# Graph and experts kernel: index loads reordered, routing laid into the first gather, gate applied by the experts' stage

## What is computed

```python
x = x + L0_gnn(layernorm(x))    # per edge: h[type, src] / deg[type, dst], summed at dst; + x @ W0.T + b
x = x + L0_ffn(layernorm(x))    # 8 experts, top 1, capacity 977, hidden 1024
x = x + L1_gnn(layernorm(x))    # graph convolution with normalised degrees, leaky relu
x = x + L1_ffn(layernorm(x))    # LSTM over the 6250 rows as one sequence, prefix and suffix sums
# L0_ffn, for each row:
probs = softmax(x @ gate_w + gate_b); idx = argmax(probs); prb = probs[idx]
pos = rank of the row among the rows of its expert; kept = pos < C
y = ybuf[idx, pos] * (prb * kept)          # ybuf = relu(buf @ w1 + b1) @ w2 + b2
y = nan_to_num(y, nan=0, posinf=10000, neginf=-10000)
```

## Time and profile before

| | us |
|---|---|
| median of 3 runs | 4495.27 (4494.93 to 4498.69) |
| the profiled execution | 4494.84 |
| its span | 4493.1 |
| PE / PEld busy | 3700.8 (82%) / 2830.6 (63%) |
| DVE / ACT / POOL busy | 1837.3 (41%) / 887.5 (20%) / 1631.3 (36%) |
| mean granted clock of TensorE | 0.879 |

### The profile page before, as it was taken

One profiled execution on the slowest core, in us unless ns is written; L12 is line 12 of the kernel. 1 busy time (PEld: TensorE's weight loads), 2 busy tenths in 40 slices (PEclk: granted clock), 3 DMA queues, 4 the chain that ended last, 5 costly groups with the idle time before them and its releaser, 6 DMA issues. The chain is left out here.

```text
span 4493.1 us, 64320 instructions
## 1 busy us (share of the span) xinstructions
PE 3700.8 (82%) x19849; PEld 2830.6 (63%) x19850; DVE 1837.3 (41%) x5512; ACT 887.5 (20%) x2492; POOL 1631.3 (36%) x1753
## 2 busy tenths in 40 slices
PE   3999999988878888865999865656667778999996
PEld 1444454457777777754666644555555557999996
DVE  3444420024334443444222283233344554444687
ACT  0333323310000000023111170000000002444453
POOL 1000000047777777733000036777777770000000
PEclk9999999978787777755999986788888899999998
DMA  4333333333333333332122054344455554433333
GB/s 156 121 120 123 125 116 149 147 117 111 110 110 111 111 111 110 111 122 90 62 82 80 28 158 133 107 126 136 148 152 161 174 183 156 148 111 115 108 108 107
DMA packets 213227, 545.38 MB, mean 121 GB/s; under 512 B 42897, under 2 KB 111358, under 8 KB 198119
## 3 DMA queue, kind: packets, MB, share of 16 engines
q1 hardware_dynamic: 121816, 297.98, 19.7%
q0 software_dynamic: 83344, 235.38, 17.8%
q10 hardware_dynamic: 7808, 8.92, 0.6%
HBM read 363.19 MB, written 178.51 MB: 121 GB/s over the span
## 5 line engine op out<-in xcount | busy, mean ns | idle before, releaser
L731 POOL DMA_INDIRECT a_msg<-scratch_hrel,k_rel_row x784 | 749.7, 956 | 1078.8 <-issue 1072.4
L1519 POOL DMA_INDIRECT b_msg<-scratch_gtab,k_src_row x784 | 763.2, 973 | 269.3 <-issue 263.5
L1568 PE MATMUL b_ps<-b_hit,b_msg 128*128 128x128 f32 x3136 | 492.6, 323 | 304.6 <-DMA b_msg<-scratch_gtab,k_src_row 296.4
L665 PE MATMUL r_psm<-k_w,r_xnT 128*128 128x512 f32 x1568 | 741.6, 609 | 0.9 <-ACT r_xnT L608 0.9
L834 PE MATMUL a_ps<-a_hit,a_msg 128*128 128x128 f32 x3136 | 562.9, 354 | 184.1 <-DMA a_msg<-scratch_hrel,k_rel_row 176.5
L1568 PEld LDWEIGHTS b_ps<-b_hit,b_msg 128*128 128x128 f32 x3136 | 460.9, 233 | 367.2 <-issue 299.6
L834 PEld LDWEIGHTS a_ps<-a_hit,a_msg 128*128 128x128 f32 x3136 | 522.2, 260 | 218.2 <-DVE a_hit L773 141.4
L1946 PE MATMUL l_psg<-k_hall,k_whhT 128*128 128x128 f32 x4672 | 565.8, 279 | 5.7 <-DVE k_hall L2063 5.5
L1946 PEld LDWEIGHTS l_psg<-k_hall,k_whhT 128*128 128x128 f32 x4672 | 542.9, 192 | 13.5 <-DVE k_hall L2063 5.9
L665 PEld LDWEIGHTS r_psm<-k_w,r_xnT 128*128 128x128 f32 x1568 | 278.0, 191 | 273.8 <-issue 251.8
L617 ACT COPY r_hst<-r_psm 128x512 f32<-128x512 f32 x392 | 229.6, 586 | 517.7 <-PE r_psm L665 517.5
(11 more groups left out here) (255 smaller groups left out, 3769.9 us busy)
## 6 DMA issues: line engine op xcount, KB each, us to landing
scratch_hrel<-r_hst SPq DMA_DIRECT2D x98, 1024.0 KB
l_xr<-scratch_xrow SPq DMA_DIRECT2D x146, 512.0 KB, 3.6
scratch_xrow<-n_xs SPq DMA_DIRECT2D x50, 512.0 KB, 3.2
a_msg<-scratch_hrel,k_rel_row POOLq DMA_INDIRECT x784, 2.8
b_msg<-scratch_gtab,k_src_row POOLq DMA_INDIRECT x784, 2.8
scratch_buf<-k_zpad POOLq DMA_DIRECT2D x8, 1024.0 KB, 6.6
scratch_ybuf<-x_ys POOLq DMA_DIRECT2D x8, 1024.0 KB
x_xr<-scratch_buf SPq DMA_DIRECT2D x7, 1024.0 KB, 15.1
```

What stands on the lines that cost most here:

```text
L665: mm = pe.matmul(psm[:, c % 4], xnT[:, u, kk], k.w[:, kk, c * 512:(c + 1) * 512], start=(kk == 0), stop=(kk == 1))
L731: pool.indirect_dma_start(msg[:, q, j], None, table, bass.IndirectOffsetOnAxis(ap=rows[:, g, j:j + 1].bitcast(U32), axis=0)).then_inc(s_m[ ...
L1519: pool.indirect_dma_start(msg[:, q, j], None, k.gtab, bass.IndirectOffsetOnAxis(ap=k.src_row[:, g, j:j + 1].bitcast(U32), axis=0)).then_in ...
L1568: mm = pe.matmul(ps[:, u, kk, 0:WIN], msg[:, g % SL, j, kk * P:(kk + 1) * P], hit[:, u, j], start=(j == 0), stop=(j == PER - 1))
```

## The change

**Edge stage.** The three index arrays get a semaphore each, and the DVE starts with the first. The 97-row loads are cut into 96 rows and 1 row, SP no longer waits for the memsets but for two small ones, and the relation weights go onto SP's queue behind the indices. W0 is turned here; the first four tiles of x are loaded here; ScalarE writes out every second turned block; the clearing of `k_degT`, `win_f` and the end of `k_accT` is POOL's.

```diff
-                sp.wait_ge(s_fill, 3)
                 for a, v in enumerate((dst, src, etype)):
-                    sp.dma_start(raw[0:full - H, a, 1], rows[H:full]).then_inc(s_ld, 16)
+                    sp.dma_start(raw[0:low, a, 1], rows[H:H + low]).then_inc(s_ld[a], 16)
+                    if a == 0:
+                        sp.wait_ge(s_tail, 2)
+                    sp.dma_start(raw[low:full - H, a, 1], rows[H + low:full]).then_inc(s_ld[a], 16)
...
+                for r in range(k.R):
+                    sp.dma_start(k.w[:, :, r * k.D:(r + 1) * k.D],
+                                 W_r[r].rearrange("(k p) o -> p k o", p=P)).then_inc(k.s_w, 16)
...
-                v.wait_ge(s_ld, 16 * 10)
+                v.wait_ge(s_ld[0], 16 * 4)
```

```diff
+                    for g in slots:
+                        if along and g < NG:
+                            q = g % SL
+                            if g >= SL:
+                                hold(k, pool, s_mm, g - SL + 1)
+                            for j in range(PER):
+                                pool.indirect_dma_start(
                                    msg[:, q, j], None, table,
                                    bass.IndirectOffsetOnAxis(ap=rows_of[:, g, j:j + 1].bitcast(U32), axis=0)
                                ).then_inc(s_m[q][j], 16)
+                        for b in ended(g - 10):
+                            scatter(b)
...
+                    for g in slots:
+                        if along and g + 1 < NG:
+                            weigh(g + 1)
+                        if along and g < NG:
+                            sums(g)
+                        for t in begun(g - 4):
+                            logits(t)
+                        for b in ended(g - 6):
+                            ranks(b)
+                        for t in begun(g - 3):
+                            turn(t)
+                        for t in begun(g):
+                            turn_sums(t)
...
+                    for g in slots:
+                        if along and g + 2 < NG:
+                            hot(g + 2)
+                        if along and g + 1 < NG:
+                            build(g + 1)
+                        for b in ended(g - 7):
+                            route_slots(b)
+                        for b in ended(g - 6):
+                            route_choice(b)
+                        for b in ended(g - 5):
+                            route_logits(b)
+                        for t in begun(g - 2):
+                            scale(t)
+                        for t in begun(g - 1):
+                            rows(t)
+                        if along and g < NG:
+                            add(g)
```

```diff
+                weights(act, 0)
+                weights(act, 1)
...
+                    for n in range(TB):
+                        t = TB * e + n
+                        act.wait_ge(S["yt"], t + 1)
+                        if t >= 2:
+                            act.wait_ge(S["yc"], t - 1)
+                        act.activation(yg[:, n % 2], y[:, n % 2], ACT.Copy, scale=xr[:, e % 2, n, D:D + 1]).then_inc(S["yg"], 1)
...
+                    v.tensor_scalar(ys[:, n], yg[:, n % 2], 10000.0, -10000.0, ALU.min, ALU.max).then_inc(S["m"], 1)
+                    v.tensor_scalar(fin[:], yg[:, n % 2], 0.0, 0.0, ALU.mult, ALU.is_equal).then_inc(S["m"], 1)
+                    v.wait_ge(S["m"], 2 * t + 2)
+                    v.copy_predicated(ys[:, n], fin[:], yg[:, n % 2]).then_inc(S["yc"], 1)
```

```diff
                 for m in slots:
-                    if 0 <= m - 1 < NT:
-                        norm(m - 1)
                     if 0 <= m - 3 < NT:
                         table(m - 3)
                     if 0 <= m - 2 < NT:
                         turn(m - 2)
                     if m < NT:
                         root(m)
-                    if m + 2 < NT:
-                        weigh(m + 2)
+                    if 0 <= m - 1 < NT and (m - 1) % 2 == 1:
+                        norm(m - 1)
```

More of the change, by code:

```diff
@@ L169, in _ @@
                 ins.then_inc(s_fill, 1)
[L171 to L178, removed]
+                pool.wait_ge(s_fill, 5)
@@ new lines, in _, with out_of @@
+                pe.wait_ge(s_bad, 4)
+                pe.matmul(psw[:, 1, 0:2], k.ones[:, :], bad[:], start=True, stop=True).then_inc(s_pe, 1)
+            def out_of(n):
+                return (k.dstf, srcf, k.typf)[n // PER][:, :, n % PER]
+            @block.scalar
+            def _(act):
+                act.dma_start(w0raw[:], W0_w.rearrange("(a p) i -> p a i", p=P)).then_inc(s_w0, 16)
+                with nc.allow_non_contiguous_dma("one bias of each column"):
+                    act.dma_start(k.biasT[:], W0_b.rearrange("(a p) -> p a", p=P)).then_inc(s_w0, 16)
+                for u in range(4):
+                    act.dma_start(k.xt[:, u], x[u * P:(u + 1) * P]).then_inc(k.s_x[u], 16)
+                act.activation(warm[:], k.eps[:], ACT.Sqrt).then_inc(s_wc, 1)
+                act.wait_ge(s_wt, 2)
+                act.copy(k.w0[:], psw[:, :, 0:k.D]).then_inc(s_wc, 1)
+                for n in range(1, 3 * PER, 2):
+                    act.wait_ge(s_tp, n + 1)
+                    act.copy(out_of(n), ps[:, 1, 0:NG]).then_inc(s_ev1, 1)
+                act.wait_ge(s_ev1, 3 * PER // 2)
@@ L235, in _ @@
+                v.wait_ge(s_ev1, 3 * PER // 2)
                 link(v.tensor_tensor(k.rel[:], k.dstf[:],
@@ new lines, in stage_first @@
+    cuts = [a for a in range(0, NT - 8, 8)] + [NT - 3, NT]
+    batches = list(zip(cuts[:-1], cuts[1:]))
+    NW = max(b - a for a, b in batches)
+    assert NW <= 8
+    batch_of = [i for i, (a, b) in enumerate(batches) for _ in range(a, b)]
+    s_p, s_mm, s_add, s_wt, s_th, s_t0, s_t1 = (k.sem("a_" + n) for n in ("p", "mm", "add", "wt", "th", "t0", "t1"))
+    s_t = (s_t0, s_t1)
+    s_m = [[k.pool_dma_sem(f"a_m{u}{j}") for j in range(PER)] for u in range(SL)]
+    nm = ("tok", "ld", "x0", "x1", "x2", "x3", "tp", "a", "st", "var", "std", "rec", "nm", "xn", "t2", "xt", "lg",
+          "rt", "ex", "pe", "sl")
@@ L1097, in stage_experts @@
-def stage_experts(k, b1, w2, b2, w1):
+                        v.tensor_copy(k.slot_write[:, lo:hi], cut(t3)).then_inc(S["sl"], 1)
+                        link(v.scalar_tensor_tensor(out=cut(slot), in0=cut(slot), scalar=-float(k.EX * k.CS), in1=cut(kept),
+                                                    op0=ALU.add, op1=ALU.mult))
+                        link(v.tensor_scalar(cut(slot), cut(slot), float(k.EX * k.CS), None, ALU.add))
+                        link(v.tensor_copy(k.slot_read[:, lo:hi], cut(slot)))
@@ L1099, in stage_experts @@
+        for_windows(k, "a_", scan, ended=lambda: tiles(False), fixed=lambda: tiles(True), flag=k.late)
+def stage_experts(k, w1, b1, w2, b2):
     nc, D, EX, CS = k.nc, k.D, k.EX, k.CS
```

847 lines of the change are left out of this document (441 added, 406 removed).

## The result

The changed kernel takes 4344.6 us (median of 4, 4341.9 to 4354.2) against 4495.7 for the kernel before: ratio 0.9667, 95% interval 0.965 to 0.9683. Forecast was 4344, in a range of 4324 to 4388. The profiled execution took 4344.8, span 4343.0, so the 150.1 us by which the span fell (4493.1 to 4343.0) can be laid out stage by stage.

A forecast was written before the change was run, and what follows sets the result against it. Transfers bound the edge, TensorE relations and experts, POOL both gathers, a chain of small steps routing, VectorE combine. Terms -47 - 89 + 4 - 19 = -151 from 4494.8 gave 4344 us, range 4324 to 4388.

The forecast's parts named there:

- Edge: Edge stage: split index loads, indices ahead of weights and an earlier start bring the first relation matmul forward, -47 us.
- Routing in the gather: First gather and route stage: routing laid beside the gather costs 50.8 + 2 there and saves 141.9 behind it, -89 us.
- the tail: Between the gather's last add and the experts' first load: routing work left for the last tiles, 27.1 us.
- The 1056-byte rows: Scatters: rows of 1056 instead of 1024 bytes taken as free, at worst 0.3 us each, +12 us.
- R1: Rival, first gather: POOL waits for its scatters' inputs or is slowed by neighbours, +36 us, 4380 us; chance 0.18.
- The sign of error that the prediction named: First gather: POOL's line showing waits for slot_write or TensorE's sums of more than some 10 us.
- Experts: Experts' stage: later start +2.5 us (0 to +8), nothing in the loop, end +1.6, together +4 us.
- Combine: Combine stage: VectorE loses clip, test and select, so a tile falls from 2.34 to 1.96 us, -19 us.
- The ring: Combine stage: copy of turned tile, product, table, copy again becomes the bound at 1.96 us a tile.
- R2: Rival, edge stage: the 96-row loads stay slow, +23 us, 4367 us; chance 0.05.
- R3: Rival, first gather: chained waits of fixed slot order make TensorE the bound in the last third, +65, 4409 us; chance 0.07.
- R4: Rival, first gather: POOL's pauses drop TensorE's clock to 1.2 GHz throughout, +199 us, 4543 us; chance 0.02.

The follow-up runs named there:

- the second pair: The kernel before and the changed kernel, both unchanged, run again on one chip: 4498.5 and 4348.5 us, ratio 0.9659.
- before_same: The kernel before, unchanged, run again as a run of its own: 4498.5 us, ratio 0.9996.
- after_same: The changed kernel, unchanged, run again beside the kernel before on the same chip: 4348.5 us, ratio 0.9659.
- e_degT_late: The changed kernel with GpSimd's memset of the degree table moved behind VectorE's third index cast: first relation matmul at 39.7 us instead of 40.9.
- c_turn_first: The changed kernel with the next tile's turning put ahead of the last product on TensorE and ScalarE in the combine stage: 4803.6 us, combine stage 115.3.
- x_second_late: The changed kernel with the second expert's weights and rows loaded only after the first expert's rows are turned: 4804.2 us, first product after 13.1.

## Why the prediction was right

- **Edge, -47 forecast, -44.3.** The mechanism is the one told. That 97 rows made the loads slow is shown by undoing the split: 18.2 us for what the prediction priced at 23. Order has a price too (12.7 on SP's queue), but what the old order cost was not measured. Mis-sized is "the twelve turned blocks are out by about 19": it was 22, and the list of VectorE ended at 31.8 instead of 29. The step that failed is the memset that "costs nothing" on GpSimd: it held VectorE's first cast for 4 us (4.82 instead of 0.69). Only 1.2 to 1.5 us of this reach the end, since VectorE then waits for the first edges, the source rows and the types, and meets the memset in another cast. The last step (8.6 us to the first matmul) took 9.1.
- **Routing in the gather, -89 forecast, -88.0.** 40 x 1.27 + 2 = 52.8 against 53.0 (56.0 in the second pair); the tail 27.1 against 28.0 from the end of the last add. The 1056-byte rows cost at most 10 ns in a scatter (981 against 971 on the mean). The gathers went from 956 to 959 ns, 1.9 us in all, as the 2 us taken for neighbours; the bound of 13 was not reached. Slots of the in-gather batches were ready in time, as forecast (R1 not seen). The sign of error that the prediction named, more than some 10 us of waits for `slot_write`, does appear (22.2 us), but both waits lie in the tail, where the 27.1 us had priced them. On the chips where the gather took 1330 us this step's premise, GpSimd without a gap, does not hold.
- **Experts, +4 forecast, +8.4 (and +8.0 between before_same and after_same).** The term that was mis-sized is the start, +2.5 taken from 0 to 8, measured +7.4 and +5.4. I let 1 MB of w1 and 1 MB of rows share the rate; ScalarE's queue carries w2 right behind w1, and the rows are eight loads that land in 6.9 us (median) instead of 2.6. Which of the two matrices delays them was not tried. What is left of the stage, 1.0 and 2.6 us, fits the 1.6 that the prediction put on its end and nothing in the loop; the two were not read apart.
- **Combine, -19 forecast, -25.2 (-21.0 in the second pair).** The ring is there to the figure: 1.96 us a tile. Mis-sized is the pitch of before outside its steady part: from first to last row add it took 115.3 us for 48 tiles, 2.40 each and not 2.34, and after it 92.9, 1.94. That and the first tile's 1.7 make 24 of the 25. In the second pair the same 48 tiles took 115.0 and 95.3, and the whole gain was 21.0, so up to 4 of the 6 us above the forecast are scatter.
- **R2** needed 96-row loads as slow as 97-row ones; they were not. **R3 and R4** did not occur where the forecast was made: granted clock 0.76 and 6.7 us of GpSimd's waits for TensorE. On chips A and B the gather's granted clock was 0.67 (e_degT_late, 907 to 2224 us) and it lost some 275 us against 1055. R4 had priced the lower clock alone at +199. In e_degT_late TensorE was busy for 956 us there instead of 856, so 100 us are longer matmuls, and the rest is idle time of which the cause is open. What the change is worth there, the variants nearest to it tell (e_degT_late, c_turn_first, x_second_late): ratios of 0.9795 to 0.9811, some 98 us instead of 151.

## What to carry to other kernels

Price work that moves beside a bound engine by the instructions which it puts into that engine's own queue: here, where GpSimd was the bound, 40 issues of 1.27 us were 50.8 of the 53 us, while 73 us of VectorE and 43 of TensorE cost no more than the other 2 (5 in the second pair). Look at the row count of each load that is slow for its bytes, and at what GpSimd runs while VectorE casts. Measure on more than one chip: the change was worth 151 us on one, and variants of it about 98 on two others. When an engine is relieved, read off the stage's own drain which ring comes next, and after reordering that one expect the one behind it.

## What the hardware did that I had not expected

- A memset of 5.42 us on GpSimd held two casts of VectorE until it was over (0.69 to 4.82 us, 0.25 to 1.22), while copies out of PSUM beside it kept 0.50; a small memset behind it was held by the cast in turn (0.10 to 0.53).
- The same program, the kernel before, took 4496 to 4500 us on some chips and 4874 to 4902 on others; one of these gave 4875 and 4874 at two times. In the changed kernel and its variants the difference lies in the two gathers (1055 to 1327 and more, 1031 to 1187 and more) and a little in the combine stage (113 to 115 against 121 and more), the stages in which GpSimd issues indirect DMAs; relations agree within 2 us, experts within 3, the LSTM within 4. In the gather all engines have gaps there that no row explains, on TensorE between single matmuls of one group, as in e_degT_late:

```profile
1122.74 0.28 PEld L969 LDWEIGHTS a_ps<-a_hit,a_msg 128*128 128x128 f32 x1 [0.62 <-issue]
1123.43 1.07 PE L969 MATMUL a_ps<-a_hit,a_msg 128*128 128x128 f32 x3 [1.01 <-issue]
...
1126.24 0.57 PE L969 MATMUL a_ps<-a_hit,a_msg 128*128 128x128 f32 x1 [1.04 <-issue]
```

  What makes them was not found.
